# A two-layer convolution kernel: in the last 1x1 convolution, loads, sums and scalings in another order

## What is computed

```
def _L1_conv_ref(x, Wt, Wp, Wg, Wz, gn_w, gn_b):
    t = einsum('oc,bchw->bohw', Wt, x)
    p = einsum('oc,bchw->bohw', Wp, x)
    g = einsum('oc,bchw->bohw', Wg, x)
    y = _rbf_kernel(t, p, g)      # att[k] = sum(a_k p^k g); y = sum_k att[k] a_k t^k, k = 0, 1, 2
    z = einsum('oc,bchw->bohw', Wz, y)
    mu = mean(z, axis=(1, 2, 3)); var = mean((z - mu) ** 2, axis=(1, 2, 3))
    return (z - mu) * rsqrt(var + EPS) * gn_w + gn_b + x
```

## Time and profile before

| | |
|---|---|
| three runs, median (lowest to highest) | 2645.32 us (2628.82 to 2649.33) |
| the profiled execution | 2640.11 us |
| its span in the trace | 2638.3 us |
| PE busy | 2333.8 us, 88% |
| DVE busy | 1561.7 us, 59% |
| ACT busy | 1233.0 us, 47% |
| POOL busy | 687.2 us, 26% |
| chain that ended last: PE, DMA, DVE, ACT | 73%, 14%, 6%, 3% |

### The profile page before, as it was taken

One profiled execution on the slowest core, in us unless ns is written; L12 is line 12 of the kernel. 1 busy time (PEld: TensorE's weight loads), 2 busy tenths in 40 slices (PEclk: granted clock), 3 DMA queues, 4 the chain that ended last, 5 costly groups with the idle time before them and its releaser, 6 DMA issues.

```text
span 2638.3 us, 29349 instructions
## 1 busy us (share of the span) xinstructions
PE 2333.8 (88%) x10316; PEld 1921.2 (73%) x10316; DVE 1561.7 (59%) x3126; ACT 1233.0 (47%) x2393; POOL 687.2 (26%) x613
## 2 busy tenths in 40 slices
PE   7999997998863699999999999999999999987730
PEld 5888886777753587888888888888888878866530
DVE  4113115446345788889888889988842244544464
ACT  5444343333222455656655565665532244444454
POOL 0000013323341344455554455555400000000000
PEclk9999998898886899999999999999999999998875
DMA  7999999999996698899899889998931111144469
GB/s 255 285 290 269 293 277 336 311 350 294 341 286 254 234 327 316 320 342 340 316 327 328 314 325 339 340 321 326 324 134 68 56 36 48 64 147 160 157 245 390
DMA packets 328012, 691.68 MB, mean 262 GB/s; under 512 B 20664, under 2 KB 170040, under 8 KB 321464
## 3 DMA queue, kind: packets, MB, share of 16 engines
q1 hardware_dynamic: 225464, 327.28, 39.1%
q0 software_dynamic: 83968, 303.80, 32.4%
q10 hardware_dynamic: 18432, 58.73, 5.6%
HBM read 443.38 MB, written 246.35 MB: 261 GB/s over the span
## 4 chain that ended last, share of the span: by engine, by line
PE 73%; DMA 14%; DVE 6%; ACT 3%; SPq 2%; issue 2%; POOL 0%; ACTq 0%; DVEq 0%
PE bank L136 20%; PE bank L138 20%; PE bank L137 20%; DMA vwide<-vb 7%; PE bank L1239 4%; PE bank L1240 4%; PE bank L1241 4%; DMA xt<-x 2%; DVE z L1183 1%; PE bank L1263 1%; DMA tb<-t 1%; DMA xin<-in_x 1%; DVE zst L1153 1%; SPq L360 1%; DMA stage<-in_wl 1%
## 5 line engine op out<-in xcount | busy, mean ns | idle before, releaser
L555 POOL DMA_INDIRECT g<-vwide,tbl x576 | 667.3, 1158 | 853.6 <-DVE a L864 402.3
L136 PE MATMUL bank<-x1h,wlh 128*128 128x512 f32 x1536 | 603.8, 393 | 2.9 <-DVE x1l L1070 2.9
L138 PE MATMUL bank<-x1h,wll 128*128 128x512 f32 x1536 | 600.9, 391 | 0.0
L137 PE MATMUL bank<-x1l,wlh 128*128 128x512 f32 x1536 | 600.3, 391 | 0.0
L880 DVE SCALAR_TENSOR_TENSOR a<-g,tbl,a 128x256 f32<-128x256 f32 x1258 | 538.3, 476 | 28.6 <-DMA g<-vwide,tbl 27.0
L574 ACT ACTIVATE g<-g,tbl 128x256 f32<-128x256 f32 x972 | 409.9, 499 | 185.2 <-DMA g<-vwide,tbl 168.9
L136 PEld LDWEIGHTS bank<-x1h,wlh 128*128 128x128 f32 x1536 | 289.3, 188 | 64.1 <-issue 3.3
L138 PEld LDWEIGHTS bank<-x1h,wll 128*128 128x128 f32 x1536 | 289.0, 188 | 62.2
L137 PEld LDWEIGHTS bank<-x1l,wlh 128*128 128x128 f32 x1536 | 289.4, 188 | 61.0
L1239 PE MATMUL bank<-w2h,o1h 128*128 128x512 f32 (+1 forms) x640 | 249.0, 389 | 68.3 <-ACT vb L627 68.3
L627 ACT ACTIVATE vb<-bank 128x512 f32<-128x512 f32 (+1 forms) x320 | 166.9, 556 | 293.8 <-DMA vwide<-vb 212.4
(11 more groups left out here) (141 smaller groups left out, 3108.3 us busy)
## 6 DMA issues: line engine op xcount, KB each, us to landing
vwide<-vb SPq DMA_DIRECT2D x128, 1152.0 KB
xin<-in_x SPq DMA_DIRECT2D x64, 512.0 KB
xf<-in_x SPq DMA_DIRECT2D x32, 1024.0 KB
x<-xf ACTq DMA_DIRECT2D x32, 1024.0 KB, 6.6
out<-z SPq DMA_DIRECT2D x128, 256.0 KB, 4.4
xb<-x SPq DMA_DIRECT2D x38, 512.0 KB, 4.0
t<-ts ACTq DMA_DIRECT2D x64, 256.0 KB
tb<-t SPq DMA_DIRECT2D x16, 1024.0 KB, 5.1
```

The source lines that it names most:

```text
L136: nc.tensor.matmul(out, wh, xh, start=first, stop=False)
L137: nc.tensor.matmul(out, wh, xl, start=False, stop=False)
L138: return nc.tensor.matmul(out, wl, xh, start=False, stop=last)
L555: pool.indirect_dma_start(slot[:].rearrange("p a c -> p (a c)"), None, d["vwide"][img], bass.IndirectOffsetOnAxis(ap=at[:, i, tap(u), 0:1] ...
```

## The change

Five edits, all in the last stage. (1) t is loaded from POOL's stream, behind its last gather, all 16 chunks; the waits are that t was stored and that `TB` is free. SP issues none. (2) `y_scale` and `y_square` stand at k = 2 to 5. (3) In DVE's loop the sums stand ahead of the statistics of the same tile. (4) ACT's `fin` of a tile stands one turn after the turn in which DVE makes its sum. (5) How many tiles of image 0 are summed up to a turn is given by `adds_by`: from the fifth tile of image 1 on, three for every two tiles, until they are four ahead of it, then one for one, all 64 by turn 60 of 64.

```
+def adds_by(x):
+    return max(0, min(64, 3 * (x - 3) // 2, x + 4))
...
-            def load_t(zc):
-                sp.wait_ge(t_out, 16 * KCP * (zc + 1))
-                at_least(sp, yl_done, KCP * zc)
-                sp.dma_start(TB[:], d["t"][zc]).then_inc(t_in, 16)
...
-                if i % KIN == 3 and CHUNKS + 2 + i // KIN < ALLC:
-                    load_t(CHUNKS + 2 + i // KIN)
...
+            pool.wait_ge(fold_done, PAIRS)
+            pool.wait_ge(g_used[0], UNITS)
+            for zc in range(ALLC):
+                pool.wait_ge(t_out, 16 * KCP * (zc + 1))
+                at_least(pool, yl_done, KCP * zc)
+                pool.dma_start(TB[:], d["t"][zc]).then_inc(t_in, 16)
...
@@ ACT
-                if zc + 1 < ALLC and k < KCP:
-                    y_scale(zc + 1, k)
-                if i == ZT + FIN_LAG - 1:
+                if zc + 1 < ALLC and 2 <= k < 2 + KCP:
+                    y_scale(zc + 1, k - 2)
+                if i == ZT + 3:
                     fin_std(0)
-                if i >= ZT + FIN_LAG:
-                    fin(i - ZT - FIN_LAG)
-            for i in range(ZT - FIN_LAG, ZT):
-                fin(i)
+                for j in range(adds_by(i - ZT - 2), adds_by(i - ZT - 1)):
+                    fin(j)
...
@@ DVE
+                for j in range(adds_by(i - ZT - 1), adds_by(i - ZT)):
+                    add_x1(j)
                 stats(i)
-                if zc + 1 < ALLC and k < KCP:
-                    y_square(zc + 1, k)
-                if i == ZT + FIN_LAG - 1:
+                if zc + 1 < ALLC and 2 <= k < 2 + KCP:
+                    y_square(zc + 1, k - 2)
+                if i == ZT + 3:
                     fin_scale(0)
-                if i >= ZT + FIN_LAG:
-                    add_x1(i - ZT - FIN_LAG)
-            for i in range(ZT - FIN_LAG, ZT):
-                add_x1(i)
```

More of the change, by code:

```diff
@@ L125 @@
 TAB_OPS = 22
-FIN_LAG = 4
+def adds_by(x):
+    return max(0, min(64, 3 * (x - 3) // 2, x + 4))
 def at_least(eng, sem, value):
@@ L316, in x1_slot @@
     def x1_slot(j):
-        return j % 2 if j < ZT // 2 else (j - ZT // 2) % len(XT)
+        return j % len(XB) if j < ZT // 2 else (j - ZT // 2) % len(XT)
     def x1_before(j):
@@ L474, in _ @@
                 else:
[L475 to L478, removed]
                     for w in range(2 + GROUPS, 6 + GROUPS):
@@ L495, in store_out @@
                 sp.dma_start(out_v[i // (KIN * CHUNKS)][:, k, n * NPX:(n + 1) * NPX], Z[i % ZRING][:]).then_inc(out_done[i % 8], 16)
-            for zc in range(1, CHUNKS + 1):
-                load_t(zc)
             for h in range(2):
                 sp.wait_ge(x1_out[h], 16 * ALLC)
-            for j in range(2):
+            for j in range(len(XB)):
                 load_x1(j)
-            load_t(CHUNKS + 1)
             for i in range(ZT):
                 store_out(i)
-                if i % 2 and i // 2 + 2 < ZT // 2 + 2:
-                    load_x1(i // 2 + 2)
-                if i % KIN == 3 and CHUNKS + 2 + i // KIN < ALLC:
-                    load_t(CHUNKS + 2 + i // KIN)
+                if i % 2:
+                    load_x1(i // 2 + len(XB))
             sp.wait_ge(z_done, IMGS * ZT)
-            for j in range(ZT // 2 + 2, ZT // 2 + len(XT)):
+            for j in range(ZT // 2 + len(XB), ZT // 2 + len(XT)):
                 load_x1(j)
```

## The result

The changed kernel took 2569.57 us (median; 2565.43 to 2577.46) beside 2644.07 us for the kernel before: a ratio of 0.9739, with a 95% interval of 0.9711 to 0.9767. The prediction was 2567, between 2547 and 2592. Its profiled execution has a span of 2567.3 us, against 2638.3.

The account below looks back on a forecast made before the run. PE bounds image 0, late `yl` image 1, DMA the end. PE's end without loss 2470.8, plus 5.5 stall, plus 86.4 end, gives span 2562.7, execution 2564.5 (2569.7 against the median); forecast 2567, range 2547 to 2592.

Parts of the forecast that it names:

- What bounds the kernel: z products: PE bounds image 0; image 1 loses 69.0 us, mainly to late `yl`; DMA bounds the end.
- t by POOL: t's loads in both images: issued as `yl` ends, landing taken as 7.2 us; up to 10.8 allowed.
- lower bound of 6.2: POOL's t load: SP's landing time of 6.2 us, taken as the least, since nothing makes the same bytes faster.
- the slower rival: `tb<-t` in every chunk: POOL's load starves beside DVE; eats the gain at 13.9 us, 2671 at 16; chance 0.04.
- Scaling two tiles later: `y_scale` now starts in place 2: 7.5 us cover t's load, and the later place costs nothing in image 0.
- Sums ahead, `fin` a turn behind: Image 1: one chain becomes two streams, DVE 17.2 and ACT 16.5 us per chunk, both under PE's 22.4.
- Three for two: Image 1's catching up: x1 late, one PE stall of 3.6 us plus clock's 1.9; 5.5 taken.
- x1 later: Rival: x1 lands later than 3.8 us beside t; two us more give stalls 11.6 and about 5, 2579; chance 0.19.
- room of 2 us: Image 1 from turn 18 on, one for one: `yl` is ready 2 us before PE's need.
- The end: After PE's last tile: SP loads `XT` at once, so 0.3 + 86.1 us remain, with DMA full.
- The sum: Whole kernel: 2476.3 + 86.4 = 2562.7 us of span, plus 1.8 around it, 2564.5; 75.6 less than the profiled execution.

Follow-up runs that it names:

- spread_ahead: Changed kernel with nine sums per eight tiles instead of three for two, and SP's x1 load ahead of the two stores: 2548.46 us, ratio 0.9680.
- all3: Changed kernel with nine sums per eight tiles, SP's x1 load ahead of the stores, and t loaded in four quarters: 2548.48 us, ratio 0.9691.
- y_early: Changed kernel with y's scaling and squares moved back two tiles, to places 0 to 3: 2561.43 us, ratio 0.9736.
- t_by_sp: Changed kernel with t loaded from SP's stream again, in image 1 behind the stores of tiles 3, 13, 21 and so on: 2566.12 us, ratio 0.9776.
- spread: Changed kernel with nine sums for eight tiles instead of three for two, all 64 again by turn 60: 2553.90 us, ratio 0.9722.

## Why the prediction was right, point by point

*What bounds the kernel.* Right. The floor of 358.2 us for z (sixteen chunks of 22.37 us and 0.3) was met to a tenth by spread_ahead and all3, and the two causes of the late `yl` were each put back or taken out alone (33.0 and 24 us).

*t by POOL.* Right in what it does, wrong in how long it takes. The trace of the changed kernel gives for the seven loads in image 1:

```profile
L561 POOL DMA_DIRECT2D tb<-t x7: 527/528/530, 2291.0 to 2440.3; - x7
...
DMA to landing us min/median/max: 5.0/7.8/8.3
```

The issue is 0.53 us, and the landing 7.8 in the median, where I had 7.2. My lower bound of 6.2 was no bound: with the DMA engines at 0.12, in image 0, t landed in 5.0 to 5.2 us. ACT waited 2.3 us in all, but 1.5 in one piece where I had said none over 1. POOL was not starved by DVE, which was busy 125 of 194 us: the longest landing is 8.3 us, and none came more than 9.7 us after the end of `yl`, far from 13.9, where the slower rival would have decided. The rule of the Trainium skill ("SBUF — State Buffer", the box on DVE blocking DMA) is about instructions that hold both ports; no run here shows it at work.

*Scaling two tiles later.* I costed its cover and gave it no gain of its own. Right: y_early shows none.

*Sums ahead, `fin` a turn behind.* Right. Two streams instead of one chain; PE waits at two borders and not at six.

*Three for two: the mis-sized term.* The mechanism, the place and the first time were right. I had put the issue of pair 2 at 24.7 to 25.1 us after tile 64's start; by the trace it begins at 25.3 (tile 64 starts at 2288.7). I then took 3.8 us for its landing, from a stage in which t was issued behind x1 on SP's own queue. (That figure already counts from the start of the issue, so the 0.4 stood in my sum twice.) It took 7.8 beside t, so DVE's sum came at 33.1 and not 28.9, and `yl` was ready at 53.5 and not 48.6: PE waited 8.29 us where I had 3.6. The next chunk, where I had found 0.6 us of room, waited 2.66. The window of image 1 took 193.9 us at a clock of 0.96, where I had looked for some 185 near 1.00. The clock's price was right as a size: 373.0 less the floor and less the two waits leaves 3.9 us, two times 1.9. In sum z was 9.3 us longer than the 363.7 that I had. I had named this as a rival, "x1 later", with a stall of 11.6 and 5 for two us more; the truth lies between the two, and so does the time. It is not that every landing was longer, as the rival has it: the two pairs beside t at 2313.8 took 7.8 and 8.4 us, the next four 3.7 to 5.0. What I held against the rival, that 325 GB/s over a chunk lie under the 388 of the end, was no argument: while pair 2 was on its way the DMA engines were busy for 0.90 of the time at 285 GB/s.

The place of DVE's waits for x1 was half wrong. I expected 15 us or more, nearly all in turns 7 to 18; of the 44.9 us, 22.0 came after 2371, in the one-for-one part, where a pair beside each load of t is late again. PE doesn't notice them, as its room of 2 us predicted.

*The end.* SP's first `XT` load came 0.02 us after PE's last matmul, and the rest took 84.4 us with DMA at 0.98, where I had 0.3 and 86.1: 2 us better than said.

*The sum.* Predicted span 2562.7, measured 2567.3. Of the difference, +9.3 is the x1 term and -2.0 the end; the remaining -2.8 is that the z products began at 2109.83 and not 2112.60, in code that the change doesn't touch. A part of the agreement is therefore luck: the terms that the change controls summed to 457.5 where I had 450.1, 7.4 us too few. The forecast of 75.6 us less stands against 68.2 by z and end, and 74.5 by the medians.

## What to carry to other kernels

When two in-order engines hand each tile to each other within one turn of a loop, their times add, as 24 us of z showed here; moving the second hand-over a turn later makes the longer of the two the bound, and it moves the wait to whatever is loaded next. A load that refills a buffer should be issued on the event that frees it, ahead of stores whose data come later: that one move of SP's loads took 9 us off z here. And work that must be caught up costs least when it is spread over all the time there is: nine for eight gave the same short end as three for two, with a z 8 us shorter.

## What the runs showed of the hardware that I had not expected

- A 512 KB load on SP's queue issued within 0.2 us of a 1 MB load on POOL's landed in 7.8 and 8.05 us; without it at its side, in 4.3. In the kernel before, where both went through SP's queue and x1 went first, the median was 3.8; in t_by_sp, on the same queue but behind t, it was 7.2 to 8.6. So what counted here is whether t's bytes were beside or ahead of the load, and hardly which engine had issued them. Splitting the 1 MB into four pieces, three of them earlier, left it at 7.5.
- PE's clock was lowered behind a wait of only 2.66 us: the window from 2369.4 to 2374.0 shows 0.63, between its levels of 1.2 and 2.4 GHz. Behind the 1.19 us at 2109.83 the stage's window shows 1.00. The length of the wait doesn't decide it alone: in t_by_sp the clock fell behind 2.12 us (0.67 below), in spread it stayed at 1.00 behind 3.00 us.

```profile
2352.90:2358.00 5.10, 5.06 (x15) 4.05 (x16) 3.15 (x5) 2.30 (x4) 0.00 (x0) 0.67 0.38 85
...
2324.10:2329.00 4.90, 4.85 (x21) 4.00 (x22) 4.90 (x8) 2.31 (x4) 0.53 (x1) 1.00 0.35 90
```

- The 1 MB of t from POOL landed in 5.1 us (median of the seven issued from 2134.7 to 2268.7) while the DMA engines were at 0.12, and in 7.8 in image 1, with DVE at two thirds of its time and DMA at 0.61.
